# Fused attention blocks on one core: two slots instead of one between a pair's projection and its maxima

## The chip, the cores and the metric

The kernel runs on one core of a Trainium2 chip. The metric is device time in microseconds (us) of one execution. The engines carry these names in the profile: PE is TensorE (PEld its weight loads), DVE is VectorE, ACT is ScalarE, POOL is GpSimd, SP issues most DMAs.

## What is computed

The input `x` is 8 sequences of 256 rows by 160, the context 8 sequences of 512 rows by 96. A first block (an adapter with two attentions) is followed by a transformer block, cut here to what matters:

```
def cross_attention(x, ctx, wq, wk, wv, wo, bo):      # 20 heads of 64
    q, k, v = x @ wq, ctx @ wk, ctx @ wv              # split into heads
    attn = softmax(q @ k.T * 64 ** -0.5)
    return (attn @ v, heads joined) @ wo + bo

x = cross_attention(layer_norm(x), layer_norm(x), ...) + x    # "self": 256 keys
x = cross_attention(layer_norm(x), context, ...) + x          # "cross": 512 keys
x = geglu_ff(layer_norm(x)) + x
```

The weights of queries and keys are scaled so that the softmax needs its row maxima, and products are made of high and low parts to keep near float32 precision.

## The kernel before

`build` (L2271) runs stages one after the other: the adapter (two stages), `attention` for self (called at L2310), `attention` for cross (L2312), and `feed_forward`. The change touches only `attention` (L271) and the constant `TAIL` (L117).

`attention` treats the 8 batches in turn, and in each batch ten pairs of heads (`PAIRS`), one pair a slot. It is a software pipeline over slots. For pair `p` the steps are, each in its own slot: projection (`proj`, the queries, in self with the keys; `kproj`, the keys in cross, L753 to L770), maxima (`find_max`, L785 in cross and L790 in self: scores once, only to be reduced), `mt` (L850: the maxima transposed), `score` (L803 and L809: scores minus maxima, transposed, in high and low parts), and `weigh` (L829 to L831: probabilities times values in four groups, each one head and half of the rows). The line `MAX, MT, SCORE, WEIGH = 1, 2, 3, 4` (L284) says how many slots behind the projection each step comes. The slots of one batch run on into those of the next; `periods` (L98) writes out the kinds of batch: first, a hardware loop of six steady ones, two written out in each turn, last, and a tail of `TAIL` slots.

In self there are 256 keys and one round in a slot (`ROUNDS`, L281), in cross 512 keys and two. A round begins with `find_max` and `score` for their pairs; what follows is the list that `items` (L318) makes for a slot: (round, step). The extras that `extras` (L300) names are units of work that are not a pair's own: `ot` (L741, outputs of two pairs transposed), `out` (L750, L752: the output projection of half the rows), `v` (L735, a group of 512 or 256 value columns), `ctx` (L712, transposed context), `ln` (L718, transposed normalised rows of the next batch). `VALUES` (L296) places the `v` units. The first extra of a slot stands between weigh groups 0 and 1, the others between groups 2 and 3. In self both places are in the one round, in cross in the first and in the second.

The other engines walk the same lists in the same order:

- ACT (L559): exponentials (L567) of the scored round, then a copy of each unit's high part out of PSUM: `turned` (L557) for `mt`, `qk_h` (L552) for `proj` and `kproj`, `v_h` (L541), `attn_th` (L544), `ctx_h` (L537), and for `ln` the scaled rows (L521, L522).
- VectorE (L653): the reduction of the maxima (L664) first; in slot 4 the normalised rows `xn` of the next batch (`normalise`, L599 and L601, four pieces); then the low part of each unit: `qk_l` (L650), `v_l` (L629), `attn_tl` (L634), four operations for `ln` (L614 to L618), two additions for `out` (L641, L643); in slot 3 the statistics (L587 to L592); last the division of the weighed values by their sums (`recip` L680, `attn` L683).
- GpSimd (L483): in slot 4 the inverse root for the next batch (L473, L475) and the output bias (L488), then the low part of the probabilities (`probs_l`, L496), one operation a round.

What binds them are semaphores. `find_max` of a pair waits until VectorE has written its `qk_l` (`projected_by`, L349). The first weigh group waits for `probs_l` of its pair and for `attn` of the pair before, as they share a PSUM bank. The units `mt`, `proj`, `kproj` and all extras go through a ring of three shared PSUM banks (`Ring`, L40): a unit may start when the one three places before it has been read. `qk_h`, `qk_l` and `attn` keep four pairs (`KEPT`).

The order within a slot stands in this function:

```
if (s >= MT and cur) or (s < MT and kind != "first"):
    out.append((0, ("mt", s)))
if cur:
    out.append((0, ("proj", s)))
weigh = (s >= WEIGH and cur) or (s < WEIGH and kind != "first")
out += [(0, ("weigh", 0))] * weigh
out += [(0, key) for key in more[:1]]
out += [(0, ("weigh", 1))] * weigh
if cross and cur:
    out.append((last, ("kproj", s)))
```

Of the kernel before, what the change touches and what calls it, by code (L numbers as in the profile page):

```python
# [97 lines left out]
def periods(engine, slot):  # L98
# [11 lines left out]
    for s in range(PAIRS):  # L110
        slot("last", s, (NB - 1, 1), (NB - 2, 0), None)
    for s in range(TAIL):
        slot("tail", s, None, (NB - 1, 1), None)

TAIL = 7  # L117


def load_stacked(engine, out, w, semaphore):  # L120
# [150 lines left out]
def attention(nc, name, cross, x, ident, ctx_dram, weights, background):  # L271
# [9 lines left out]
    ROUNDS = KT // 2  # L281
    RB = ROUNDS * PAIRS

    MAX, MT, SCORE, WEIGH = 1, 2, 3, 4  # L284
    KEPT = 4

    def kept(parity, p):
# [12 lines left out]
    def extras(kind, s):  # L300

        out = []
        has_prev, has_nxt, has_cur = kind != "first", kind in ("first", "steady"), kind != "tail"
        if has_prev and s in (1, 2, 4):
            out.append(("ot", "prev", 2 + s // 2))
        if cross and has_nxt and s == 4:
            out.append(("ctx", "nxt", 0))
        if has_nxt and s == 4:
            out.append(("ln", "nxt", 0))
        if has_prev and s in (5, 6):  # L310
            out.append(("out", "prev", s - 5))
        if has_cur and s in (7, 9):
            out.append(("ot", "cur", s // 2 - 3))
        out += [("v", "nxt", v) for v in (VALUES[0].get(s, ()) if has_nxt else ())]
        out += [("v", "cur", v) for v in (VALUES[1].get(s, ()) if has_cur else ())]
        return out

    def items(kind, s):  # L318

        cur, more = kind != "tail", extras(kind, s)  # L320
        last = ROUNDS - 1
        out = []
        if (s >= MT and cur) or (s < MT and kind != "first"):
            out.append((0, ("mt", s)))
        if cur:
            out.append((0, ("proj", s)))
        weigh = (s >= WEIGH and cur) or (s < WEIGH and kind != "first")
        out += [(0, ("weigh", 0))] * weigh
        out += [(0, key) for key in more[:1]]
        out += [(0, ("weigh", 1))] * weigh  # L330
        if cross and cur:
            out.append((last, ("kproj", s)))
        out += [(last, ("weigh", 2))] * weigh
        out += [(last, key) for key in more[1:]]
        out += [(last, ("weigh", 3))] * weigh
        return out

    def all_keys(kind):
        if kind == "tail":
            return [key for s in range(TAIL) for _, key in items(kind, s) if key[0] != "weigh"]  # L340
        pre = []
        if kind == "first":
            pre = [("ctx", "pre", 0)] * cross + [("ln", "pre", 0)] + [("v", "pre", v) for v in range(AHEAD)]
        return pre + [key for s in range(PAIRS) for _, key in items(kind, s) if key[0] != "weigh"]
# [18 lines left out]
    with stack:  # L363
# [153 lines left out]
        def _(act):  # L517
# [41 lines left out]
            def slot(kind, s, cur, prev, nxt):  # L559
                period = cur[0] if cur is not None else NB  # L560
                for r in range(ROUNDS):
                    if (work := before(s, SCORE, cur, prev)) is not None:
                        (b, _), p = work
                        n = p * ROUNDS + r
                        act.wait_ge(scored, b * RB + n + 1)
                        after(act, pv_done, b * PAIRS + p - 1)
                        nc.scalar.activation(probs[:, n % PR, :, :].rearrange("p j k -> p (j k)"), score_bank[:, :], ACT.Exp,  # L567
                                             scale=SCALE).then_inc(exped, 1)
                    for at, key in items(kind, s):
                        if at != r or key[0] == "weigh":  # L570
                            continue
                        if key[0] == "mt":
                            turn_shift(kind, period, key, before(s, MT, cur, prev))
                        elif key[0] in ("proj", "kproj"):
                            projected(kind, s, cur, key)
                        else:
                            extra(kind, period, key, {"cur": cur, "prev": prev, "nxt": nxt}[key[1]])
# [1693 lines left out]
def build(nc, columns, shapes, a, out):  # L2271
# [5 lines left out]
    with stack:  # L2277
        x = stack.enter_context(nc.sbuf_tensor("x_rows", [P, NT, HID], F32))
        ident = stack.enter_context(nc.sbuf_tensor("ident", [P, P], F32))
        with ExitStack() as self_stack:  # L2280
            self_weights = SelfWeights(nc, self_stack, {w.rstrip("1"): l1[w] for w in ("g1", "be1", "wq1", "wk1", "wv1", "wo1", "bo1")})
            with ExitStack() as adapter_stack:
# [25 lines left out]
                adapter(nc, x, const, context, raw, branch)  # L2308
            cross_weights = CrossWeights(nc, stack, {w.rstrip("2"): l1[w] for w in ("g2", "be2", "wq2", "wk2", "wv2", "bo2")})
            attention(nc, "self", False, x, ident, context, self_weights, cross_weights)  # L2310
        late = LateRaw(nc, stack, {"wo": l1["wo2"], "w1": l1["w_ff1"]})
        attention(nc, "cross", True, x, ident, context, cross_weights, late)  # L2312
        feed_forward(nc, x, ident, l1["g3"], l1["be3"], l1["b_ff1"], l1["b_ff2"], l1["w_ff2"], late, out)

# [14 lines left out]
```

## Time and profile before

| | us |
|---|---|
| median of 3 runs | 1677.85 (1672.35 to 1679.42) |
| the profiled execution, its own time | 1676.27 |
| its span | 1674.5 |
| mean granted clock of TensorE, share of full | 0.939 |
| busy: PE, PEld | 1465.7 (88%), 1236.4 (74%) |
| busy: DVE, ACT, POOL | 1101.1 (66%), 747.4 (45%), 734.6 (44%) |

The self-attention lies between about 436 and 884 us of the span, the cross-attention between 884 and 1563, the feed-forward behind it. The time of an execution is 1.8 us more than the span of its profile.

How to read the rows: a timeline row is start, duration, engine, line, operation, what is written from what, the shape and the count of instructions merged, and in brackets how long the engine had been idle and whom it waited for. A wait row names the waiting engine and line, the releaser, the total, the number of times and the longest. A window row gives the busy us of each engine with its number of instructions, then the granted clock. A matmul's duration is longer than the distance to the next one, since they are pipelined; distances are taken from start to start.

### The profile page before, as it was taken

Reading aid. Unit: us, or ns where it says so; the run is one execution under the profiler, and the core shown is the slowest. Engines: PE = TensorE matmul, PEld = TensorE weight load, DVE = VectorE, ACT = ScalarE, POOL = GpSimd, SP = SyncE. Lnnn points to the kernel's source line nnn. Section 1 sums busy time; section 2 is a strip of 40 time slices with the busy share of each in tenths; the row PEclk is TensorE's granted clock in tenths of the full one; section 3 lists DMA queues with packets and bytes.
Section 4 is the critical chain, followed back from the end, with each engine's and each line's share of the span. In section 5 each row is a group of like instructions: output and inputs, shape, how many; then the busy total and the mean of one; then the engine's idle time right before and its main releaser. Section 6 shows DMA issues by size and latency. Waiting matters only on the chain. (4 is left out here: it accounts for less than half of the span.)

```text
span 1674.5 us, 42467 instructions
## 1 busy us (share of the span) xinstructions
PE 1465.7 (88%) x16742; PEld 1236.4 (74%) x16742; DVE 1101.1 (66%) x2091; ACT 747.4 (45%) x1365; POOL 734.6 (44%) x576
## 2 busy tenths in 40 slices
PE   4786899999589999899986999999998999998487
PEld 3564777777478888788875788878887888887477
DVE  3773677776467766767646776766685767665376
ACT  0442344444244544445532554545454545554243
POOL 1341355556444443434432554544454545445154
PEclk9865899999799999999997999999999999999699
DMA  3110000000200000000001000000000000000000
GB/s 94 48 37 12 9 7 10 5 1 2 57 1 2 2 2 2 2 2 2 2 2 34 7 2 7 6 3 3 7 24 18 2 2 2 2 2 2 12 13 20
DMA packets 23427, 19.51 MB, mean 12 GB/s; under 512 B 12962, under 2 KB 21638, under 8 KB 23238
## 3 DMA queue, kind: packets, MB, share of 16 engines
q1 hardware_dynamic: 23238, 16.83, 3.8%
q8 instruction: 139, 2.28, 0.5%
q14 instruction: 50, 0.41, 0.1%
HBM read 15.51 MB, written 1.31 MB: 10 GB/s over the span
## 5 line engine op out<-in xcount | busy, mean ns | idle before, releaser
L496 POOL TENSOR_TENSOR cross_probs_l<-cross_probs 128x1024 f16<-128x1024 f32 x160 | 303.3, 1896 | 337.2 <-ACT cross_probs L567 337.2
L567 ACT ACTIVATE cross_probs<-cross_score 128x1024 f32<-128x1024 f32 x160 | 164.0, 1025 | 278.3 <-PE cross_score L809 278.3
L496 POOL TENSOR_TENSOR self_probs_l<-self_probs 128x1024 f16<-128x1024 f32 x80 | 151.6, 1895 | 242.1 <-ACT self_probs L567 242.0
L664 DVE TENSOR_REDUCE cross_maxima<-cross_max 128x2 f32<-128x1024 f32 x160 | 195.0, 1219 | 10.1 <-PE cross_max L785 7.9
L1982 POOL TENSOR_TENSOR ad_probs_l<-ad_probs 128x512 f16<-128x512 f32 (+1 forms) x128 | 133.7, 1045 | 124.1 <-ACT ad_probs L2028 123.8
L650 DVE TENSOR_TENSOR cross_qk_l<-cross_shared,cross_qk_h 128x256 fp32r<-128x256 f32 (+1 forms) x160 | 89.0, 556 | 122.4 <-ACT cross_qk_h L552 122.3
L829 PE MATMUL cross_pv<-cross_v_h,cross_probs 128*128 128x65 bf16 x1280 | 149.8, 197 | 7.6 <-DVE cross_attn L683 4.3
L829 PEld LDWEIGHTS cross_pv<-cross_v_h,cross_probs 128*128 128x128 bf16 x1280 | 116.9, 98 | 46.7 <-issue 37.9
L830 PE MATMUL cross_pv<-cross_v_l,cross_probs 128*128 128x64 f16 x1280 | 147.3, 194 | 0.0
L831 PE MATMUL cross_pv<-cross_v_h,cross_probs_l 128*128 128x65 bf16 x1280 | 146.6, 194 | 0.0
L567 ACT ACTIVATE self_probs<-self_score 128x1024 f32<-128x1024 f32 x80 | 82.3, 1029 | 141.9 <-PE self_score L809 141.9
L830 PEld LDWEIGHTS cross_pv<-cross_v_l,cross_probs 128*128 128x128 bf16 x1280 | 120.0, 99 | 0.5
L2028 ACT ACTIVATE ad_probs<-ad_score 128x512 f32<-128x512 f32 (+1 forms) x128 | 76.5, 598 | 97.8 <-PE ad_score L2219 97.8
L831 PEld LDWEIGHTS cross_pv<-cross_v_h,cross_probs_l 128*128 128x128 f16 x1280 | 119.9, 99 | 0.0
L785 PE MATMUL cross_max<-cross_qk_h 64*128 64x512 f32 x320 | 80.6, 500 | 31.9 <-DVE cross_qk_l L650 25.8
L650 DVE TENSOR_TENSOR self_qk_l<-self_shared,self_qk_h 128x512 fp32r<-128x512 f32 x80 | 55.2, 690 | 71.0 <-ACT self_qk_h L552 71.0
L664 DVE TENSOR_REDUCE self_maxima<-self_max 128x4 f32<-128x1024 f32 x80 | 97.3, 1217 | 3.7 <-PE self_max L790 3.5
L809 PE MATMUL cross_score<-cross_qk_h 64*128 64x256 f32 x640 | 92.1, 281 | 0.0
L809 PE MATMUL cross_score<-cross_qk_l,cross_qk_h 64*128 64x256 f32 x640 | 92.1, 281 | 0.0
L809 PE MATMUL cross_score<-cross_qk_h,cross_qk_l 64*128 64x256 f32 x640 | 91.8, 279 | 0.0
L2103 DVE TENSOR_REDUCE ad_maxima<-ad_max 128x1 f32<-128x508 f32 x128 | 84.2, 681 | 3.6 <-PE ad_max L2205 1.9
L829 PE MATMUL self_pv<-self_v_h,self_probs 128*128 128x65 bf16 x640 | 78.9, 197 | 6.9 <-DVE self_attn L683 6.7
(441 smaller groups left out, 5042.6 us busy)
## 6 DMA issues: line engine op xcount, KB each, us to landing
ad_ctx_rows<-in_ctx SPq DMA_DIRECT2D x8, 192.0 KB, 2.6
cross_ctx_rows<-in_ctx SPq DMA_DIRECT2D x8, 192.0 KB, 2.6
x_rows<-in_x SPq DMA_DIRECT2D x1, 1280.0 KB, 6.3
sw_raw<-in_L_xattn_wq SPq DMA_DIRECT2D x2, 640.0 KB, 6.0
sw_raw<-in_L_xattn_wk SPq DMA_DIRECT2D x2, 640.0 KB, 3.7
sw_raw<-in_L_xattn_wv SPq DMA_DIRECT2D x2, 640.0 KB, 3.6
cw_raw<-in_L_xattn_wq SPq DMA_DIRECT2D x2, 640.0 KB, 4.6
lr_raw<-in_L_xattn_w_ff SPq DMA_DIRECT2D x2, 640.0 KB
```

The lines of the kernel that those rows point to most:

```text
L496: nc.gpsimd.tensor_tensor(probs_l[:, n % PR, :, :].rearrange("p j k -> p (j k)"), whole, whole.bitcast(BF16)[:, 1::2], ALU.subtract).then_ ...
L567: nc.scalar.activation(probs[:, n % PR, :, :].rearrange("p j k -> p (j k)"), score_bank[:, :], ACT.Exp, scale=SCALE).then_inc(exped, 1)
L650: nc.vector.tensor_tensor(qk_l[:, kept(parity, s), at:at + width], shared[ring.bank(kind, key)][:, 0:width], qk_h[:, kept(parity, s), at:a ...
L664: nc.vector.reduce_max(out, scores, AX.X).then_inc(max_read, 1)
L785: mm = nc.tensor.matmul(max_bank[:, j * 512:(j + 1) * 512], qk_h[half, at, r * P:(r + 1) * P], qk_h[half, at, SEQ:SEQ + KD], start=True, s ...
L809: mm = nc.tensor.matmul(score_bank[:, j * 512 + c * SEQ:j * 512 + (c + 1) * SEQ], ks[half, at, keys], qs[half, at, 0:SEQ], start=False, st ...
L829: nc.tensor.matmul(pv_bank[:, at:at + DV], hi, v_h[parity][:, c, head, :], start=c == 0, stop=False)
L830: nc.tensor.matmul(pv_bank[:, at:at + DH], hi, v_l[parity][:, c, head, :], start=False, stop=False)
L831: mm = nc.tensor.matmul(pv_bank[:, at:at + DV], lo, v_h[parity][:, c, head, :], start=False, stop=last)
L1982: nc.gpsimd.tensor_tensor(probs_l[rows, n % PR, :], whole, whole.bitcast(BF16)[:, 1::2], ALU.subtract).then_inc(probs_split, 1)
L2028: nc.scalar.activation(probs[rows, n % PR, :], score_bank[n % 2][rows, :], ACT.Exp, scale=SCALE).then_inc(exped, 1)
L2103: nc.vector.reduce_max(maxima[:, v % 2, step % 2, at:at + 1], max_bank[n % 2][:, 0:KEYS], AX.X).then_inc(max_read, 1)
```

## The change

The distances become 2, 3, 4 and 5, so that every step behind the projection comes a slot later, and the tail has eight slots. The extras `ot` and `out` move to the slots in which their pairs are now ready; `ctx`, `ln` and the `v` units keep their slots. In `items` the projection `proj` moves from the place behind `mt` to the one ahead of weigh group 2, in cross into the second round, ahead of `kproj`. The whole diff:

```diff
--- before.py
+++ after.py
@@ -114,7 +114,7 @@
 
 
 
-TAIL = 7
+TAIL = 8
 
 
 def load_stacked(engine, out, w, semaphore):
@@ -281,7 +281,7 @@
     ROUNDS = KT // 2
     RB = ROUNDS * PAIRS
 
-    MAX, MT, SCORE, WEIGH = 1, 2, 3, 4
+    MAX, MT, SCORE, WEIGH = 2, 3, 4, 5
     KEPT = 4
 
     def kept(parity, p):
@@ -301,16 +301,16 @@
 
         out = []
         has_prev, has_nxt, has_cur = kind != "first", kind in ("first", "steady"), kind != "tail"
-        if has_prev and s in (1, 2, 4):
-            out.append(("ot", "prev", 2 + s // 2))
+        if has_prev and s in (2, 3, 5):
+            out.append(("ot", "prev", (s + 3) // 2))
         if cross and has_nxt and s == 4:
             out.append(("ctx", "nxt", 0))
         if has_nxt and s == 4:
             out.append(("ln", "nxt", 0))
-        if has_prev and s in (5, 6):
-            out.append(("out", "prev", s - 5))
-        if has_cur and s in (7, 9):
-            out.append(("ot", "cur", s // 2 - 3))
+        if has_prev and s in (6, 7):
+            out.append(("out", "prev", s - 6))
+        if has_cur and s in (8, 9):
+            out.append(("ot", "cur", s - 8))
         out += [("v", "nxt", v) for v in (VALUES[0].get(s, ()) if has_nxt else ())]
         out += [("v", "cur", v) for v in (VALUES[1].get(s, ()) if has_cur else ())]
         return out
@@ -322,14 +322,14 @@
         out = []
         if (s >= MT and cur) or (s < MT and kind != "first"):
             out.append((0, ("mt", s)))
-        if cur:
-            out.append((0, ("proj", s)))
         weigh = (s >= WEIGH and cur) or (s < WEIGH and kind != "first")
         out += [(0, ("weigh", 0))] * weigh
         out += [(0, key) for key in more[:1]]
         out += [(0, ("weigh", 1))] * weigh
-        if cross and cur:
-            out.append((last, ("kproj", s)))
+        if cur:
+            out.append((last, ("proj", s)))
+            if cross:
+                out.append((last, ("kproj", s)))
         out += [(last, ("weigh", 2))] * weigh
         out += [(last, key) for key in more[1:]]
         out += [(last, ("weigh", 3))] * weigh
```

In slot 4 of a steady batch the lists of steps behind maxima and scores become, in self: before `mt, proj, weigh 0, ot 4, weigh 1, weigh 2, ln, weigh 3`, after `mt, weigh 0, ln, weigh 1, proj, weigh 2, weigh 3`; in cross: before `mt, proj, weigh 0, ot 4, weigh 1 | kproj, weigh 2, ctx, ln, weigh 3`, after `mt, weigh 0, ctx, weigh 1 | proj, kproj, weigh 2, ln, weigh 3`, where | divides the rounds.

## Rows read from the trace of the kernel before

**Rows 1.** busy us (count) of each engine in one self batch, then granted clock
```profile
core 0: us, PE busy (x) PEld busy (x) DVE busy (x) ACT busy (x) POOL busy (x), PEclk, DMA share, GB/s
541.09:592.66 51.57, 47.99 (x610) 43.24 (x610) 36.52 (x69) 25.80 (x43) 20.70 (x14) 1.00 0.01 2
```

**Rows 2.** who waited for whom: us in total, times, longest; whole run
```profile
PE cross_max L785 <- DVE cross_qk_l L650: 25.8, 38, 1.8
...
PE self_shared L718 <- DVE self_xn L601: 18.7, 8, 5.2
...
PE self_max L790 <- DVE self_qk_l L650: 15.2, 30, 1.4
...
PE self_pv L829 <- DVE self_attn L683: 6.7, 8, 1.5
```

**Rows 3.** timeline of TensorE, self-attention, slots 3 to 5 of one batch; columns named
```profile
start us, us, engine line op out<-in xcount [idle before <-releaser]
...
566.61 0.28 PE L757 MATMUL self_shared<-self_ln_h,sw_wk_s 128*128 128x256 f32 x1
...
568.37 0.51 PE L790 MATMUL self_max<-self_qk_h 64*128 64x256 f32 x4 [0.73 <-DVE self_qk_l L650]
...
569.94 0.37 PE L757 MATMUL self_shared<-self_ln_h,sw_wq_h 128*128 128x256 f32 x1
...
573.58 0.65 PE L718 MATMUL self_shared<-ident,self_xn 128*128 128x128 f32 x4 [1.44 <-DVE self_xn L601]
...
577.89 0.19 PE L829 MATMUL self_pv<-self_v_h,self_probs 128*128 128x65 bf16 x1 [0.81 <-DVE self_attn L683]
```

**Rows 4.** timeline of VectorE, the same slots
```profile
567.54 0.69 DVE L650 TENSOR_TENSOR self_qk_l<-self_shared,self_qk_h 128x512 fp32r<-128x512 f32 x1 [0.97 <-ACT self_qk_h L552]
...
569.15 0.42 DVE L683 TENSOR_TENSOR self_attn<-self_pv,self_recip 128x256 f32<-128x256 f32 x1
...
570.96 1.98 DVE L601 TENSOR_SCALAR self_xn<-x_rows,self_mean_var,self_rstd 128x128 f32 x1
...
577.32 0.42 DVE L683 TENSOR_TENSOR self_attn<-self_pv,self_recip 128x256 f32<-128x256 f32 x1
```

**Rows 5.** timeline of TensorE, first tail slot of the self-attention
```profile
861.26 0.50 PE L790 MATMUL self_max<-self_qk_h 64*128 64x256 f32 x4 [0.18 <-DVE self_qk_l L650]
...
862.91 0.19 PE L829 MATMUL self_pv<-self_v_h,self_probs 128*128 128x65 bf16 x1
```

**Rows 6.** timeline of both engines, self slot after one that ends in a V group
```profile
550.98 0.50 PE L790 MATMUL self_max<-self_qk_h 64*128 64x256 f32 x4
...
551.51 0.69 DVE L629 TENSOR_TENSOR self_v_l<-self_shared,self_v_h 128x512 f16<-128x512 f32 x1 [0.68 <-ACT self_v_h L541]
...
552.32 0.42 DVE L683 TENSOR_TENSOR self_attn<-self_pv,self_recip 128x256 f32<-128x256 f32 x1
```

**Rows 7.** timeline of both engines, the same place in the cross-attention
```profile
1312.85 0.50 PE L785 MATMUL cross_max<-cross_qk_h 64*128 64x512 f32 x2
...
1313.98 0.42 DVE L683 TENSOR_TENSOR cross_attn<-cross_pv,cross_recip 128x256 f32<-128x256 f32 x1
```

**Rows 8.** timeline of GpSimd, slot 4 of rows 3
```profile
570.96 1.89 POOL L496 TENSOR_TENSOR self_probs_l<-self_probs 128x1024 f16<-128x1024 f32 x1
```

**Rows 9.** timeline of both engines, cross-attention, slots 4 and 5
```profile
1078.04 0.50 PE L785 MATMUL cross_max<-cross_qk_h 64*128 64x512 f32 x2 [0.30 <-DVE cross_qk_l L650]
...
1079.15 0.42 DVE L683 TENSOR_TENSOR cross_attn<-cross_pv,cross_recip 128x256 f32<-128x256 f32 x1
...
1083.65 0.67 DVE L634 TENSOR_TENSOR cross_attn_tl<-cross_shared,cross_attn_th 128x512 fp32r<-128x512 f32 x1
...
1086.18 0.49 PE L785 MATMUL cross_max<-cross_qk_h 64*128 64x512 f32 x2 [0.75 <-DVE cross_qk_l L650]
...
1088.56 0.42 DVE L683 TENSOR_TENSOR cross_attn<-cross_pv,cross_recip 128x256 f32<-128x256 f32 x1
...
1089.13 0.19 PE L829 MATMUL cross_pv<-cross_v_h,cross_probs 128*128 128x65 bf16 x1 [0.63 <-DVE cross_attn L683]
```

**Rows 10.** windows as in rows 1: a pause of TensorE and what follows it
```profile
602.50:605.10 2.60, 0.15 (x5) 0.03 (x1) 1.20 (x3) 0.58 (x1) 0.00 (x0) 0.99 0.00 0
605.10:608.50 3.40, 3.33 (x23) 3.02 (x23) 1.23 (x1) 0.71 (x1) 0.00 (x0) 0.51 0.02 5
```

## The prediction

> **What bounds the kernel now.** I read the page's busy shares first, then the table of windows, the waits, and the timelines of single slots. In one batch of the self-attention TensorE is busy 47.99 of 51.57 us at full clock, VectorE 36.5, GpSimd 20.7 [rows 1]; the batches in the middle of a stage repeat each other to a few hundredths, so one slot read closely stands for its sisters. TensorE sets the time, but only where it does not wait, and its waits have three names [rows 2]. For the maxima of a pair it waits for VectorE's low parts (`qk_l`, L650) of the projection issued one slot earlier: 15.2 us in 30 waits in self, 25.8 us in 38 in cross. For the transposes of the next batch's normalised rows (`ln` unit, L718) it waits for VectorE's L601: 18.7 us, 8 times. For the first weigh group it waits for VectorE's `attn` of the pair before: 6.7 us, 8 times in self.
>
> Slot 4 of a self batch shows all three [rows 3]: maxima at 568.37 after 0.73 us idle, the `ln` transposes at 573.58 after 1.44, the next slot's first weigh at 577.89 after 0.81. VectorE is the releaser each time [rows 4]: `qk_l` ends at 568.23, `attn` at 569.57, the second `xn` piece takes from 570.96 to 572.94, `attn` of slot 4 ends at 577.74. So VectorE's order inside slots 3 to 5 is a chain as tight as TensorE's.
>
> **What the change removes.** With two slots between projection and maxima, `qk_l` is ready a whole slot ahead. The two rows together are 41.0 us. Start to start a wait costs a little more: after the last projection matmul at 566.61, the 24 weigh matmuls (0.03 us each) and two hand-overs of 0.12 would put the maxima at 567.56, so 0.81 is lost where the row says 0.73. Scaled so, the gain is **46 us** (bounds 41 and 48); about 9 of it lies in the two stage starts.
>
> **What it adds: the weigh group comes sooner.** TensorE's matmuls are the same in number, but the order in a slot changes from mt, proj, weigh to mt, weigh, proj. Today the projection (about 1.0 us in self: eight matmuls from 569.94 to the weigh) covers VectorE's `attn` of the slot before. Now nothing does. The tail of self already has the new order: maxima at 861.26, first weigh at 862.91, 1.65 us later [rows 5]; with a projection next it starts 1.57 us after the maxima (568.37 to 569.94). When can `attn` be ready? Where a 512-wide V group is last in a slot, slot start 550.98, `v_l` from 551.51, `attn` ends at 552.74: 1.76 us, and 0.15 more to the weigh (577.74 to 577.89), so 1.91 against 1.57: **0.34** lost in two slots of a self batch. Where the projection is last, its last matmul starts 1.62 us before `qk_l` ends (566.61, 568.23), `attn` ends 0.54 after the DVE operation ahead of it (552.20 to 552.74 [rows 6]), plus 0.15: 2.31 after that matmul; TensorE needs 0.12 + 0.36 + 0.09 + 1.57 = 2.14 from it, so **0.17** in some four slots. With 0.13 and 0.08 for the two others outside slots 3 to 5, a self batch pays 1.6 us: 6 x 1.6 and 2.9 for the first and last batch are **12.5 us**. Below nothing is excluded, since no matmul goes; the upper end is 20 if every slot paid 0.3. In cross the V-last case is milder: slot start 1312.85, `attn` ends at 1314.40, 1.55 + 0.15 against 1.56: 0.14 in four slots [rows 7]; the key projection is followed by twice the weigh work and waits for nothing; the five other slots pay the changed hand-over of 0.09. That is 1.0 us a batch, **8 us** in all (0 to 12).
>
> **The `ln` unit is moved, though the diff doesn't name it.** `ot` unit 4 goes from slot 4 to slot 5. In self `ln` was the second extra of slot 4, after weigh 2; now it is the first and goes right behind weigh 0, before the projection. VectorE's chain to `xn` does not get shorter: `qk_l` of slot 3, statistics, GpSimd's root, reduce, four normalising pieces, one of them held for 1.98 us beside GpSimd's `probs_l`, which starts at the same 570.96 [rows 4, 8]. Count from E, the end of slot 3's projection (566.89): `attn` ends at E+2.68, `ln` can start at E+6.69. After the change slot 4 starts at E+0.29, its first weigh is due at E+1.86 and comes at E+2.83 (0.97 lost), and `ln` is due at E+3.01 and comes at E+6.69: 3.68 lost where 1.61 is now. Behind it stand weigh 1, the projection, weigh 2 and 3 and all of slot 5. On VectorE `ln` now stands before the projection's low part: from `ln` to the end of `attn` it is 4.16 now (573.58 to 577.74) and 4.76 with 0.6 of `qk_l` between, so slot 5's weigh comes at E+11.6 against a due time of E+10.33: 1.27 lost, 0.97 now. Together 0.97 + 2.07 + 0.30 = 3.34 us a batch, six steady batches, and 0.5 in the first: **20.5 us** (bounds 10, should only the `ln` wait grow and by what the moved `ot` and projection took, 0.55 + 1.0; and 25).
>
> In cross `ctx` takes the first place and `ln` stays behind weigh 2, where `xn` is long ready, so that wait doesn't come. But the q projection's low part moves into the second round, VectorE's chain in slot 4 loses only `ot` (0.6), and TensorE arrives earlier. `attn` of slot 3 ends at 1079.57, the weigh may start at 1079.72; the slot would start 0.38 before 1078.04, the weigh is due at 1079.22: 0.5. `attn` of slot 4 would end at 1088.38 instead of 1088.98, the weigh comes at 1088.53; TensorE, 0.8 us of wait and `ot`'s 0.44 shorter, is due some 1.9 earlier. 0.5 + 1.9 against what stands now before 1089.13 (0.63 in the row, 0.8 start to start) is +1.6 a batch, **10.5 us** over six and the first [rows 9] (5 to 13).
>
> **Queues passed.** ACT copies in the new order and has no late item; the shared banks are claimed three units back, and every such bank was emptied before `attn`, which is waited for anyhow: nothing. No DMA moves. The tail grows by one slot in each attention, its matmuls taken from the slot before; the bubbles of one thin slot, 1 us each (0.3 to 1.7, by the waits of the present tails): **2 us**.
>
> **The clock.** After TensorE's pause of 2.6 us (602.50 to 605.10) its granted clock is 0.51 for the next 3.4 us, which is the 1.2 GHz level [rows 10]. The new pause at `ln` is 0.97 and 3.68 us with one weigh group of 0.18 between. At half clock 3.4 us lose 1.7 us, most of it inside the 1.27 that slot 5 waits anyway: 0.5 a batch, **3 us** (0 to 16). The Trainium skill, page TensorE: Matmul & The Clock Gate, section Why this matters for your kernels, says that idle gaps between bursts put the clock back to its low level; by that rule each of these pauses would be followed by slow matmuls, which is the rival below.
>
> **Sum.** -46 + 12.5 + 8 + 20.5 + 10.5 + 2 + 3 = +10.5 on the profiled execution's 1676.27. The gains in the stage starts are the least certain and I put them 2 higher, since two slots without maxima also ease VectorE: 1684.8. The median shown is 1.6 above the profiled execution, so 1685 to 1686; I take **1685**. About 0.5% (8 us) is what a measurement of this kernel can tell from no change.
>
> **Rivals.**
> *Slower, by the clock.* Place: the `ln` unit in slot 4 of each self batch. If the pause there pulls the clock down and slot 5 runs at the low level too, past its slack of 1.27, each of six batches pays some 2 us more: 1685 + 12 = 1697. For it speaks that a shorter pause does it now [rows 10]; against it that the present pauses at `ln` don't, and that much of the slow time is covered. It decides if the pause reaches about 2.6 us. Chance 0.24.
> *Faster, by a missed collision.* The long `xn` piece and `probs_l` both start at 570.96 [rows 4, 8]. If after the change VectorE's piece starts first, it takes a third of a us instead of 1.98, and both chains of slot 4 shorten by 1.65 in 12 batches: 1685 - 20 = 1665. Against it: both engines are released by the same statistics, so their distance stays. The Trainium skill, page SBUF — State Buffer, section Who interferes with whom, says that whichever engine starts first holds the shared ports for its whole instruction and the other blocks; by that rule this near tie could fall either way. Chance 0.15.
> *The whole gain.* VectorE keeps up everywhere and only 46 - 8 us remain: 1638. Rows 4 and 9 speak against it. Chance 0.04.
> *The forecast*, 1677 to 1693, has 0.57: its bounds are the terms' ends taken half-way.
>
> **Numbers.** Of the forecast's 0.57 some 0.34 lies within 0.5% and 0.23 above; the clock's 0.24 is slower; of the collision's 0.15, 0.11 is faster and 0.04 same; the whole gain is faster. That is 0.15 faster, 0.38 same, 0.47 slower. The range 1668 to 1700 holds the forecast and the clock's rival and leaves out the whole gain and about half of the collision's.
>
> **What would show it.** The maxima's waits for `qk_l` go to nearly nothing. L718's wait in self rises from 18.7 to about 35 us, the weigh's wait for `attn` from 6.7 to over 20 in self, and by 15 or more in cross. A self batch takes about 54.9 us instead of 51.57, a cross batch half a us to one more. I am wrong if L718 waits no longer than now, if self batches get shorter, or if the clock column drops in every batch.

## The result and the profile after

The kernel after takes 1681.76 us (median of 20 runs, 1676.31 to 1688.69) where the one before, run beside it, takes 1674.55 (20 runs, 1666.05 to 1681.0): a ratio of 1.0043, with a 95% interval of 1.0029 to 1.0057. That is slower by 0.43%, inside the 0.5% that the prediction called no change. The profiled execution took 1677.53 us, its span 1675.7, against 1676.27 and 1674.5: it is one of the quick ones of the kernel after, so the two profiles lie 1.3 us apart where the medians lie 7.2 apart. From its page, the busy times and the granted clock:

```profile
PE 1487.7 (89%) x16742; PEld 1247.4 (74%) x16742; DVE 1097.7 (66%) x2091; ACT 747.5 (45%) x1365; POOL 733.9 (44%) x576
...
PEclk9995899999799999999997899999999999999799
```

Nearly equal totals hide two stages that moved against each other. A stage is read here from its first `ln` transposes (self) or the end of self (cross) to its last output addition (L643); a batch is the distance from the `ln` unit (L718) of one batch to that of the next, taken within one turn of the hardware loop.

| us | before | after | difference |
|---|---|---|---|
| self stage | 444.7 | 460.0 | +15.3 |
| one self batch | 51.7 | 55.5 | +3.8 |
| cross stage | 682.9 | 668.1 | -14.8 |
| one cross batch | 79.9 | 78.9 | -1.0 |

The rest of the profile, adapter and feed-forward, differs by 0.8 us. A stage total is that of one execution and carries a few us of chance (the same self took 464.5 in e1 below, the same cross 672.3 in e2); a batch inside a turn of the loop repeats to 0.2 us in these two kernels, and one that crosses a turn is 2 to 6 us longer. Where in a stage the difference arises, from the starts of the `ln` units:

| us, after minus before | start | steady batches | end |
|---|---|---|---|
| self (start: to the second `ln`; end: from the last) | -7.0 | +17.4 | +4.9 |
| cross (start: to the third `ln`; end: from the last) | -9.9 | -2.7 | -2.2 |

So two thirds of what cross gains lies in its first batches and not in the steady ones: there eight waits for `qk_l`, 6.5 us, are gone, and one wait of a V unit for `v_l` fell from 5.0 to 1.5. In self the start gains 7.0, with four waits for `qk_l`, 4.3 us in all, shrunk to one of 0.5. The batches as windows (columns as in [rows 1]), first of the kernel before:

```profile
629.21:680.92 51.71, 48.11 (x608) 43.27 (x609) 36.51 (x69) 25.81 (x43) 20.70 (x13) 1.00 0.01 2
1170.11:1250.02 79.91, 76.72 (x997) 65.00 (x995) 56.44 (x96) 41.18 (x70) 39.62 (x24) 1.00 0.02 4
```

and of the kernel after:

```profile
629.85:685.32 55.47, 51.12 (x608) 45.12 (x609) 36.66 (x68) 25.22 (x43) 20.63 (x13) 0.96 0.01 1
1175.47:1254.42 78.95, 76.68 (x1000) 64.68 (x996) 56.41 (x96) 41.67 (x71) 39.58 (x24) 1.00 0.03 6
```

The work is the same (matmul counts agree to a few records). In self TensorE's busy time grew by 3.0 at a clock of 0.96; in cross it did not grow and the idle time shrank from 3.2 to 2.3. The waits of the kernel after, to be held against [rows 2]:

```profile
PE self_shared L718 <- DVE self_xn L601: 29.7, 8, 4.9
PEld self_shared L718 <- issue: 21.3, 6, 3.6
PEld self_pv L829 <- issue: 18.5, 58, 0.9
...
PE cross_pv L829 <- issue: 8.9, 6, 1.5
...
PE self_pv L829 <- DVE self_attn L683: 6.1, 8, 1.5
```

Both `qk_l` rows of [rows 2], 41.0 us, are gone. The wait for `xn` rose from 18.7 to 29.7. The weigh's wait for `attn` did not rise by name in self; the weight loads' "issue" did, from 13.5 in 34 waits to 18.5 in 58, and in cross there are six pauses of 1.5 that bear no name. That is how this page shows a wait whose releaser it can't tie to the instruction: the timeline has to say whose it is. TensorE in slots 4 and 5 of a self batch, then VectorE and GpSimd in the same slots, as in [rows 3, 4, 8]:

```profile
566.32 0.50 PE L790 MATMUL self_max<-self_qk_h 64*128 64x256 f32 x4
...
568.84 0.19 PE L829 MATMUL self_pv<-self_v_h,self_probs 128*128 128x65 bf16 x1 [0.71 <-DVE self_attn L683]
...
572.62 1.11 PE L718 MATMUL self_shared<-ident,self_xn 128*128 128x128 f32 x4 [3.44 <-DVE self_xn L601]
...
577.95 0.19 PE L829 MATMUL self_pv<-self_v_h,self_probs 128*128 128x65 bf16 x1
```

```profile
570.05 1.93 DVE L601 TENSOR_SCALAR self_xn<-x_rows,self_mean_var,self_rstd 128x128 f32 x1
...
577.42 0.42 DVE L683 TENSOR_TENSOR self_attn<-self_pv,self_recip 128x256 f32<-128x256 f32 x1
```

```profile
570.00 1.89 POOL L496 TENSOR_TENSOR self_probs_l<-self_probs 128x1024 f16<-128x1024 f32 x1
```

The weigh waits 0.71, the `ln` transposes wait 3.44, and the first weigh of slot 5 waits for nothing that is marked: TensorE itself comes late, since the four transposes took 1.11 us where they take 0.65 in [rows 3]. The windows around them (columns as before) show the pause and the clock:

```profile
568.30:572.70 4.40, 0.42 (x7) 0.33 (x8) 4.19 (x6) 0.80 (x2) 3.52 (x4) 0.94 0.00 0
572.70:576.10 3.40, 3.40 (x30) 3.28 (x30) 1.23 (x3) 1.26 (x3) 0.00 (x0) 0.58 0.00 0
576.10:578.50 2.40, 2.40 (x34) 1.98 (x31) 2.32 (x6) 1.22 (x2) 0.00 (x0) 1.00 0.01 3
```

A granted clock near 0.5 is the 1.2 GHz level; before the fall TensorE had paused 3.44 us. In cross, the same places as [rows 9]:

```profile
1085.70 0.19 PE L829 MATMUL cross_pv<-cross_v_h,cross_probs 128*128 128x65 bf16 x1 [0.68 <-DVE cross_attn L683]
...
1094.45 0.19 PE L829 MATMUL cross_pv<-cross_v_h,cross_probs 128*128 128x65 bf16 x1 [1.49 <-issue]
```

Elsewhere in a cross batch the first weigh group starts 1.64 to 1.73 us behind the slot's first maxima, so it loses at most 0.09 us.

### The profile page after: what moved, and what is told of

The parts are those of the page before. It is cut to its first block and busy times, and to the rows that moved or that the text cites. A ratio compares the mean times of both kernels' runs of the same rounds, so it can differ in the third digit from the quotient of the medians.

```text
span 1675.7 us, 42451 instructions
## 1 busy us (share of the span) xinstructions
PE 1487.7 (89%) x16742; PEld 1247.4 (74%) x16742; DVE 1097.7 (66%) x2091; ACT 747.5 (45%) x1365; POOL 733.9 (44%) x576
## 5 line engine op out<-in xcount | busy, mean ns | idle before, releaser
L829 PE MATMUL self_pv<-self_v_h,self_probs 128*128 128x65 bf16 x640 | 87.2, 198 | 7.3 <-DVE self_attn L683 6.1
```

Of the source, the lines that this page charges most:

```text
L829: nc.tensor.matmul(pv_bank[:, at:at + DV], hi, v_h[parity][:, c, head, :], start=c == 0, stop=False)
```

## The experiments

Ratios are to the kernel before, run on the same chip. "Self" and "cross" are the stages and batches as defined above.

| run | median | ratio [95%] | self, batch | cross, batch |
|---|---|---|---|---|
| e1 change in self only | 1692.18 | 1.0098 [1.0071, 1.0125] | 464.5, 55.5 | 685.7, 79.9 |
| e2 change in cross only | 1662.53 | 0.9922 [0.9895, 0.9948] | 443.6, 51.7 | 672.3, 79.0 |
| e3 self's `ln` back | 1671.66 | 0.9987 [0.9966, 1.0008] | 453.7, 54.4 | 669.2, 78.9 |
| e4 self's projection back | 1656.25 | 0.9882 [0.9857, 0.9907] | 443.3, 52.2 | 669.8, 79.0 |
| e5 e4, statistics earlier | 1659.95, one run | none | 435.1, 50.4 | 675.8, 79.0 |
| e6 e5, normalising first | 1639.32 | 0.9784 [0.9763, 0.9806] | 412.3, 47.9 | 671.8, 79.6 |
| e7 before, with e6's moves | 1664.38 | 0.9921 [0.9898, 0.9943] | 431.5, 50.0 | 686.4, 80.0 |
| e8 after, with e6's moves | 1664.31 | 0.9922 [0.9900, 0.9943] | 440.7, 52.1 | 676.4, 79.5 |
| e9 e6's moves in self only | 1633.91 | 0.9763 [0.9736, 0.9789] | 413.9, 47.9 | 671.4, 78.9 |
| e10 both projections back | 1696.48 | 1.0146 [1.0115, 1.0177] | 440.0, 52.2 | 710.3, 83.3 |
| e11 e6, `ln` ahead of `ctx` | 1633.81 | 0.9765 [0.9736, 0.9795] | 415.2, 47.9 | 671.7, 78.3 |
| e12 e9, q behind `mt`, 5 kept | 1627.72 | 0.9720 [0.9696, 0.9743] | 415.4, 47.9 | 664.4, 78.3 |

A cross stage differs between profiles by a few us with an equal batch (668.1 to 675.8 at 78.9 to 79.0), by pauses at the turns of the hardware loop and at its first batch. So a claim about cross rests on the batch, and its total only where the difference is larger.

**e1 and e2, the two halves alone.** The distances, extras, tail and order follow a switch:

```diff
-    MAX, MT, SCORE, WEIGH = 2, 3, 4, 5
+    FAR = not cross          # e2: FAR = cross
+    TAIL = 8 if FAR else 7
+    MAX, MT, SCORE, WEIGH = (2, 3, 4, 5) if FAR else (1, 2, 3, 4)
```

> The change made in the self-attention alone, the cross-attention as before. Stage lengths in the two traces: self 444.7 us before and 460.0 after, cross 682.9 and 668.1. My theory (two separate effects that cancel): self stays at 460 (459 to 461), cross at 683, the whole some 15 us over the kernel before, ratio about 1.009. Rival (the stages share a cause, such as code placement or the clock): self comes out well under 460 or cross moves by more than 3 us though nothing in it is edited.

> The change made in the cross-attention alone, the self-attention as before. My theory: self 445 us, cross 668 us (667 to 670), the whole some 15 us under the kernel before (about 1660, ratio 0.991). Rival: the gain in cross is an effect of what self left behind, and cross stays over 675.

Self alone is slower by 1.0%, cross alone faster by 0.8%: the whole change is the sum of two clear effects of opposite sign (the product of the ratios is 1.0020, which the intervals do not part from 1.0043). The batches are those of the kernel after whatever the other attention does, 55.5 and 79.0. The stage totals missed the ranges expected: self 464.5 where 459 to 461 was, cross 672.3 where 667 to 670 was, and in e1 the unedited cross came out 2.8 longer. So such a total is not to be read closer than 5 us.

**e3, the moved `ln` unit.** Only self's `ln` goes back behind weigh 2:

```diff
+        if more and more[0][0] == "ln":
+            more = [None] + more
-        out += [(0, key) for key in more[:1]]
+        out += [(0, key) for key in more[:1] if key]
```

> The changed kernel with the ln unit of self put back behind weigh 2, where it stood before. My theory: the normalised rows come when VectorE's chain has them, so TensorE's total wait in slots 4 and 5 is set by that chain; what is won is the 0.6 us of the projection's low part that stood between ln and attn, and some 0.4 us of half-clock matmuls: 1.0 us in each of six steady batches, a batch 54.5 instead of 55.5, self 454 (452 to 456). Rival (the position of ln costs the whole 2.1 us of longer wait): 3 us a batch, self 442. Second rival (the clock's drops are the loss, 17 us more at half clock in self): they vanish and self falls by 8 or 9.

The pause before `ln` fell from 3.44 to 2.06 us and the batch by 1.1. So the place of `ln` alone is worth some 6 us of the stage; the rest of self's loss is elsewhere. The clock still fell after some of these pauses, though not after all. Windows behind the `ln` of two batches, each after a pause of 2.06 to 2.08 us:

```profile
678.10:681.50 3.40, 3.40 (x30) 3.02 (x30) 2.06 (x5) 1.19 (x3) 0.00 (x0) 0.63 0.00 0
734.38:737.80 3.42, 2.58 (x30) 2.10 (x30) 2.09 (x5) 2.18 (x4) 0.06 (x1) 1.00 0.00 0
```

The fall cost this kernel nothing: its batches inside a turn take 54.45 and 54.33 us with a fall (`ln` at 511.05 and 623.77) and 54.44 without (at 734.38). In the last, the first weigh of slot 5 waits 1.69 us for `attn`; where the clock fell it waits 0.29 to 0.46, since TensorE comes to it later.

**e4, the order of projection and weigh in self.** Self's `proj` returns to the place behind `mt`, the distances stay:

```diff
+        if cur and not cross:
+            out.append((0, ("proj", s)))
...
         if cur:
-            out.append((last, ("proj", s)))
+            if cross:
+                out.append((last, ("proj", s)))
             if cross:
                 out.append((last, ("kproj", s)))
```

> The changed kernel with self's projection put back behind mt, ahead of the weigh groups; cross as changed. It covers attn again and puts 1.0 us of matmuls ahead of ln. My theory: the small waits of the weigh groups (0.14 to 0.27 us in seven slots) go, 1.4 us in each of eight batches, and the ln wait falls by 1.0 to 1.4 us in six: self 460 to about 441 (438 to 446), a steady batch 52.7. Rival (the small waits were bought from elsewhere, since the maxima or the banks then wait instead): self stays over 452.

One batch:

```profile
619.07:671.31 52.24, 49.03 (x609) 44.64 (x609) 36.58 (x69) 25.70 (x43) 20.63 (x13) 0.96 0.01 2
```

3.3 us a batch come back, 17 in the stage (441 was expected, 443.3 came). The late projection is the dearest part of the change in self. The small losses ahead of weigh 0 are gone in the slots outside 3 to 5; the `ln` pause is still 3.2 us and the clock still falls behind it.

**e5 and e6, VectorE's chain to `xn`.** e5 adds to e4 the statistics in slot 2 and the inverse root in slot 3, e6 also moves the four normalising pieces ahead of slot 4's reduction of the maxima, both in both attentions:

```diff
-                if s == 4 and nxt is not None:
+                if s == 3 and nxt is not None:
                     inverse_root(nxt[0])
...
-                if s == 3 and nxt is not None:
+                if s == 2 and nxt is not None:
                     statistics(nxt[0])
...
                 for r in range(ROUNDS):
+                    if s == 4 and r == 0 and nxt is not None:      # e6
+                        normalise(nxt[0])
                     if (work := before(s, MAX, cur, prev)) is not None:
...
-                    if s == 4 and r == 0 and nxt is not None:      # e6
-                        normalise(nxt[0])
```

> The kernel of e4_proj_first with VectorE's statistics moved from slot 3 to slot 2 and GpSimd's inverse root from slot 4 to slot 3; the four normalising pieces stay behind the reduction of slot 4. My theory (what holds the rows back is the piece that stands still beside GpSimd's probs_l, not the statistics): VectorE reaches the pieces earlier, but probs_l starts about 2.5 us into the slot and runs 1.9, so one piece of about 1.9 us stays and the ln wait of 3.1 us falls by 0.3 only (0 to 0.8): self 441 (437 to 443). Rival (the length of the chain counts): the wait falls by the 1.7 us that the chain is shorter, self 431.

> As e5_pf_early, with the four normalising pieces also put ahead of the reduction of slot 4, where GpSimd is not yet at probs_l. My theory: no long piece is left in self, the ln wait of 3.1 us goes to under 0.5, and in cross VectorE's chain in slot 4 is short enough that the 1.65 us wait of slot 5's weigh goes: self 425 (422 to 430), cross 656 (652 to 661), the whole about 1625. Rival (VectorE's order merely passes the wait on to the reduction, attn or the maxima): self stays over 435.

e5 gained 1.8 a batch, more than the theory and less than the rival: one piece still took 1.92 us beside `probs_l`. Here a fall of the clock does cost: the batches inside a turn take 51.40 us with one (`ln` at 513.57) and 50.41 and 50.42 without (at 620.57 and 726.38), and slots 3 to 5 take 16.6 to 16.7 in three batches with a fall (`ln` at 513.57, 564.97 and 670.98) and 15.74 in the two without. The first weigh of slot 5 waits only 0.4 us without a fall, so little of the slow stretch is covered. In e6 all pieces are short. Its VectorE and GpSimd:

```profile
557.21 0.34 DVE L602 TENSOR_SCALAR self_xn<-x_rows,self_mean_var,self_rstd 128x128 f32 x1
557.46 0.34 DVE L604 TENSOR_SCALAR self_xn<-x_rows,self_mean_var,self_rstd 128x128 f32 x1
557.72 0.34 DVE L602 TENSOR_SCALAR self_xn<-x_rows,self_mean_var,self_rstd 128x128 f32 x1
557.97 0.34 DVE L604 TENSOR_SCALAR self_xn<-x_rows,self_mean_var,self_rstd 128x128 f32 x1
```

```profile
556.44 0.87 POOL L491 TENSOR_TENSOR x_rows<-x_rows,sw_bo_row 128x320 f32 x1
558.46 1.89 POOL L499 TENSOR_TENSOR self_probs_l<-self_probs 128x1024 f16<-128x1024 f32 x1 [1.15 <-ACT self_probs L570]
```

But for 0.1 us the pieces fall between two operations of GpSimd's, and they end 0.15 us before `probs_l` starts. The Trainium skill, page SBUF — State Buffer, section Who interferes with whom, has VectorE and GpSimd share a port pair that the first to start holds; the 1.93 against 0.34 us of the same piece, with and without `probs_l` beside it, agree. Self's batch, 47.9, has 0.4 us of idle time left:

```profile
608.76:656.65 47.89, 47.49 (x614) 43.21 (x611) 34.76 (x69) 25.68 (x44) 20.66 (x14) 1.00 0.01 2
```

That is far better than the 425 us expected (412.3). In cross the expectation (656) was wrong: the batch got 0.6 longer. The pieces now delay the reduction that the second round's maxima wait for: that wait of TensorE's rose from 2.9 us in the kernel after to 8.0.

**e7 and e8, the same moves without e4's order.** They separate the moves from the change: e7 makes them in the kernel before, e8 in the kernel after.

> The kernel before (one slot between projection and maxima) with the same move of statistics, inverse root and normalising pieces as e6_pf_norm. My theory: the ln wait (1.61 us a batch) and most of the attn wait of slot 5 (0.97) go, the waits for qk_l stay: self 432 (430 to 436), cross 672 (668 to 676). Rival (with the chain out of the way one slot of distance is as good as two): self and cross come within 3 us of e6_pf_norm.

> The changed kernel, with nothing put back but the same move of statistics, inverse root and normalising pieces. It says how much of the changed kernel's loss hung on VectorE's chain to the rows. My theory: of 5.9 us of waits in self's slots 4 and 5 some 2.6 are left, 3.3 less in six batches, self 460 to 440 (436 to 445); in cross 2.5 us a batch less, 668 to 654 (650 to 660); the drops of the granted clock at ln vanish. Rival (the small waits of the weigh groups and the clock's drops carry the loss): self stays over 450.

Self came as expected in both (431.5 for 432, 440.7 for 440). Cross missed in both: 686.4 where 672 was expected and 676.4 where 654 was, and neither batch became shorter. In e8 the `ln` pause is 0.67 us and the clock stays at 1.00 in the six batches behind it. Compared at like clocks, e8 (52.1) and e6 (47.9) price the late projection in self at 4.2 a batch; at the old distances self's best is 50.0 (e7), at the new ones with the old order 47.9. So the two slots between projection and maxima are worth 2.1 a batch in self once nothing else stands in VectorE's way. The order that the change brings along takes twice that back. (e4 gave 3.3 for the same order, with VectorE's chain to `xn` still long; that the chain took the difference is argued, not shown.)

**e9, the moves in self only.** The conditions of e6 with `cross` excepted.

> The kernel after with self's projection behind `mt` again and, in self alone, the early statistics and inverse root and the normalising pieces ahead of the reduction; cross is the change's, untouched. My theory: the two attentions are independent, so self is that of e6 (412 us, batch 47.9) and cross that of the kernel after (668, batch 78.9, 0.5 a batch less than in e6 and e8, where the moved pieces delay cross's own chain). 1639 minus about 3: near 1635, ratio to before 0.976. Rival: cross's half a us in e6 and e8 was chance of the runs; then the time is e6's, 1639 or more.

It came at 1633.91, expected near 1635. The batch of cross is 78.9 again, so the 0.6 of e6 was of the moves; the whole differs from e6 by 0.2%, within the intervals.

**e10, both projections back.** Cross's q projection too stands behind `mt`.

```diff
+        if cur:
+            out.append((0, ("proj", s)))
...
         if cur:
-            out.append((last, ("proj", s)))
             if cross:
                 out.append((last, ("kproj", s)))
```

> The kernel after with the projection behind `mt` again in both attentions; against e4 only cross's q projection goes back into the first round. It prices the later projection in cross. By my prediction's terms (8 us for weigh groups that come sooner, and the part of the 10.5 in slots 4 and 5 that comes from the q projection's low part in the second round) cross should fall from 669 to 655 to 662, the whole to 1643 to 1650. Rival, by the gaps read in the trace after, where cross's weigh groups outside slots 4 and 5 wait for nothing: no more than the share of slots 4 and 5, 0.3 to 0.9 a batch, so cross 663 to 668 and the whole 1650 to 1656.

Both theories fell: cross took 710.3, forty more than e4. Its waits name why:

```profile
DVE cross_qk_l L651 <- ACT cross_qk_h L553: 229.0, 72, 7.4
ACT cross_qk_h L553 <- PE cross_score L810: 207.8, 76, 4.4
...
PE cross_max L786 <- DVE cross_maxima L665: 41.7, 45, 1.3
```

and its ScalarE, then its VectorE, in one slot:

```profile
1025.88 0.37 ACT L558 CAST cross_turned<-cross_shared 128x256 fp32r<-128x256 f32 x1
1028.31 0.37 ACT L553 CAST cross_qk_h<-cross_shared 128x256 fp32r<-128x256 f32 x1 [2.07 <-PE cross_score L810]
```

```profile
1028.72 0.42 DVE L651 TENSOR_TENSOR cross_qk_l<-cross_shared,cross_qk_h 128x256 fp32r<-128x256 f32 x1 [2.25 <-ACT cross_qk_h L553]
...
1029.81 1.22 DVE L665 TENSOR_REDUCE cross_maxima<-cross_max 128x2 f32<-128x1024 f32 x1
```

`qk_h` keeps four pairs (`KEPT`), and ACT may overwrite pair p - 4 only when both rounds of its scores are done (L550). With `SCORE` at 4 these scores are in the same slot, the last of them in the second round. A projection in the first round must stand still for them on ACT, and VectorE's second reduction stands behind its low part. So in cross the move of the projection into the second half is not a choice of balance: with four pairs kept the longer distance needs it.

**e11, `ln` ahead of `ctx` in cross.**

```diff
-        if cross and has_nxt and s == 4:
-            out.append(("ctx", "nxt", 0))
         if has_nxt and s == 4:
             out.append(("ln", "nxt", 0))
+        if cross and has_nxt and s == 4:
+            out.append(("ctx", "nxt", 0))
```

> e6 with `ln` ahead of `ctx` in slot 4 of cross, so that VectorE's four operations for `ln` stand in the first round and only one operation for `ctx` stands ahead of `attn`. My theory: the 1.6 us that the first weigh group of slot 5 waits in cross is the four operations of `ln` (1.7 us) that stand between the key projection's low part and `attn`; with 1 us less there the wait falls to about 0.6 and cross by 6 to 8 us, from 671.8 to about 665. Rival: the wait comes from VectorE's whole amount of work in slots 4 and 5 (maxima 2.4, projection 1.1, ln 1.7, ctx 0.7, attn 0.6); then it moves elsewhere in the slot (the second maxima) and cross stays at 672.

The batch fell from 79.6 to 78.3, the upper end of the 1.0 to 1.3 that the expected 6 to 8 us need, so the place is right: VectorE's four operations for `ln` ahead of `attn`. The stage did not fall in this profile (671.7): the stretch behind the last `ln` is 4.8 us longer than in e6, and no run here tells why. The whole is 0.2% below e6, within the intervals. The stage total stays undecided.

**e12, five pairs of queries kept.** e9 with cross's q projection behind `mt`, and

```diff
+            q_h = sb("q_h", [P, 5, SEQ], F32R)
+            q_l = sb("q_l", [P, 5, SEQ], F32R)
...
-                after(act, scored, b * RB + (s - KEPT + 1) * ROUNDS)
+                after(act, scored, b * RB + (s - (5 if cross and key[0] == "proj" else KEPT) + 1) * ROUNDS)
...
-        attn_tl = sb("attn_tl", [P, NCH, SEQ], F32R)
+        attn_tl = sb("attn_tl", [P, NCH - cross, SEQ], F32R)
```

> e9 with cross's q projection back behind `mt`, as in e10, but with five pairs of queries kept in place of four (the keys stay at four). The fourth pair from the end of the low parts of the output projection is given up for the room in SBUF: in cross the low parts of pairs 8 and 9 are written over those of pairs 7 and 8, so that part of the result is left out; no instruction is left out. My theory: e10's 40 us came from ACT, which may copy the queries of pair p only when pair p - 4 is scored, and with three slots between them that score is in the second round of the same slot; ACT waited 207.8 us in 76 waits, and VectorE's second reduction stood behind it. With five kept the wait goes and cross falls from e10's 710 (batch 83.3) to that of the change or below: by my prediction's terms for cross (weigh groups 1.0 a batch, and 0.9 of slots 4 and 5 for the low part in the second round) a batch of 77.0 to 78.0, cross 657 to 664, the whole about 1622 to 1628. Rival one, from the gaps in the trace of the kernel after: only slots 4 and 5 gain, up to 0.8 a batch, cross 665 to 669, whole 1628 to 1633. Rival two: the kept pairs are not the cause, and cross stays near 700.

One cross batch of e10, then of e12:

```profile
1168.24:1251.57 83.33, 77.30 (x995) 65.15 (x995) 54.51 (x96) 39.91 (x71) 39.59 (x23) 1.00 0.02 4
```

```profile
1125.16:1203.50 78.34, 76.67 (x995) 64.87 (x995) 56.33 (x96) 41.36 (x71) 39.62 (x24) 1.00 0.02 6
```

5.0 a batch come back and ACT's wait for scores is gone: the kept pairs were the cause of e10. Against the order of the change (78.9) the batch gains 0.6, by the first of the two rivals that the expectation names, not the 0.9 to 1.9 of my terms: from maxima to maxima slot 4 is 0.33 longer and slot 5 0.80 shorter than in e9, and none of the eight others differs by more than 0.05. So the late projection costs cross little but what it does to slots 4 and 5. The totals don't decide this: stage and whole (664.4 and 1627.72) lie between the theory's ranges and the rival's. This kernel, 1627.72 us or 2.8% below the one before, gives up part of the result; the best with the whole result are e9 and e11, at 0.976.

## Why the prediction was right, and where it was not

The time, 1681.76 against 1685, came out, and with it the forecast's place within 0.5% of the kernel before; but the chances that stood beside it gave 0.47 to slower than that and 0.38 to the same. The mechanisms are those forecast, with one term of the wrong size and one reason that failed. That the medians differ by 7.2, where the forecast's difference was 7, is in part luck, as the sum below shows. Point by point:

- **The waits for `qk_l`** went as forecast. What they were worth is seen in cross, where little else changed: -2.83 start to start in a steady batch (0.37, 0.80 and twice 0.83).
- **The `ln` unit of self** was right in kind and size. 0.97 was forecast ahead of the first weigh of slot 4 and 3.68 ahead of `ln`. Counted as the forecast counts, from 1.57 behind the maxima (566.32 to 568.84) and from 0.18 behind the weigh (568.84 to 572.62), they are 0.95 and 3.60. Only the statement for the page was off: the wait rose to 29.7, not "about 35", and the step's own 2.07 in six batches on 18.7 gives 31.
- **The weigh term of self**, 1.6 a batch, holds. From maxima to maxima the seven slots outside 3 to 5 are longer in e8 than in e6 by 0.37, 0.18, 0.14, 0.20, 0.37, 0.24 and 0.24: 1.7 (the forecast's own terms count eight such slots). Slots 3 to 5 add 0.8, 1.0 and 0.6. But it does not stand under `attn` in the waits (forecast over 20, 6.1 came); it is "issue" and busy time. In cross the row was to grow by 15 or more: by name it is 4.1 where it was 4.3, and the six pauses without a name add 8.9.
- **The clock**: "I am wrong if the clock column drops in every batch". It did, in all six steady batches, as the rival had it. The rule of the Trainium skill that stood beside it (TensorE: Matmul & The Clock Gate, Why this matters for your kernels) speaks of long idle gaps alone, which the prediction left out. The falls behind 3.44 us here and 3.20 in e4, six of six each, agree with it; those behind 2.06 to 2.08 us in e3 and 2.35 in e5, four of six each, are behind shorter gaps than it names, and there the measurement decides. Yet the rival's price, 12 us, did not come. The slow stretch of 3.4 us lies where slot 5 would have waited for `attn` anyhow: with the first weigh at 577.95 and `attn` done at 577.84 the expected wait of 1.27 is gone. By the forecast's count from the same maxima this weigh was due at 577.63, so it comes 0.3 late: the drop took the place of a wait, and the forecast's small term held while its reason (that most batches keep their clock) failed. No run changes the clock alone, but e3 and e5 have batches with and without a fall, and they agree: where slot 5's first weigh has 1.69 us to wait a fall costs nothing (e3), where it has 0.4 a fall costs 0.8 to 1.0 (e5). In the kernel after the clock fell in all six batches, so for it this is argued. What a fall can have cost there is the 0.46 us by which the four transposes took longer, 1.11 for 0.65, as VectorE's way to `attn` leads over them.
- **The weigh term of cross**, 8 us, is the mis-sized term. Outside slots 4 and 5 the first weigh group loses 0.09 at most. The prediction took 0.14 in four slots and 0.09 for the hand-over in five others, 1.0 a batch; e12 prices the whole order of cross at 0.6 a batch, slots 4 and 5 included.
- **Slots 4 and 5 of cross**: forecast +1.6, measured 0.85, 0.18 and 1.65 in place of 0.81, which is +1.9. With -2.83 that is -0.9 a batch, and -1.0 is measured. The text, though, said that a cross batch takes "half a us to one more": its own terms, 1.0 + 1.6 and the -2.83, give -0.2. That sentence was not worked out from the sum.
- **The sum.** By the profiled stages self lost 15.3 and cross gained 14.8, where the terms make cross gain 8 to 10 (26 to 29 us of `qk_l` less 8 and 10.5) and self lose about 20 (12.5, 20.5, 3 and a tail, less 17 of `qk_l`). In these two profiles both were off by some 5 in the same direction, so the total, forecast at +8.5 on the profile, came at +1.3. In e1 and e2 the same attentions come out at +19.8 and -10.6, about as forecast, and the medians differ by +7.2: a good part of the 5 is the chance of one execution, and how near the time came is partly luck.
- **The stage starts**, put at about 9 and then 2 more, brought more: 7.0 in self and 9.9 in cross (6.9 in e1, 6.2 in e2), 13 to 17 in all. The wait of a V unit for `v_l` at the start of cross, 5.0 before and 1.5 after, stands in no term. Against this, the end of self grew by 4.9, and how that divides into the weigh term, slots 4 and 5 and the longer tail no run here shows.
- **The missed collision** did not happen: the second piece took 1.93 us and starts 0.05 after `probs_l`. Its price was right, and e6 shows that the way to it is to move the pieces, not to hope for the order of a near tie.
- Not seen at all: that `KEPT` ties the place of the projection to the distance (e10). It cost the prediction nothing, since the change keeps to it; "ACT has no late item" was true only for that reason.

## What to carry to other kernels

Moving a step later in a software pipeline buys slack at one wait and takes cover from others: list what the moved instructions used to hide (here `attn` and the chain to `xn`), and price each. When a pipeline gets longer, check every buffer that keeps a fixed number of items; a step that was free may now wait for one in its own slot. And a whole that hardly moves may be two halves that cancel: run each alone before judging the idea. Here one half was worth 0.8%; the other was worth 1% once its order was restored and VectorE's chain shortened (self 413.9 in e9 against 431.5 in e7, which has the same moves at the old distances).

## What was unexpected of the hardware

The clock's fall is not decided by the length of the pause alone. Idle time of TensorE before `ln` in the self batches behind the first, and in how many of six the clock fell to 1.2 GHz within 2 us of their end:

| kernel | pause, us | clock fell |
|---|---|---|
| before | 1.42 to 1.44 | 0 of 6 |
| e8 | 0.67 | 0 of 6 |
| e3 | 2.06 to 2.08 | 4 of 6 |
| e5 | 2.34 to 2.35 | 4 of 6 |
| e4 | 3.20 to 3.21 | 6 of 6 |
| after | 3.43 to 3.44 | 6 of 6 |

Two batches of e5, behind pauses of 2.35 us each, in the windows' columns:

```profile
564.97:568.40 3.43, 3.43 (x34) 3.17 (x36) 1.65 (x4) 1.02 (x2) 0.00 (x0) 0.53 0.01 2
620.57:624.00 3.43, 3.43 (x48) 3.18 (x49) 2.10 (x5) 1.83 (x3) 0.00 (x0) 1.00 0.00 0
```

In the same 3.43 us TensorE did 34 matmuls at the low level and 48 at the high one. The batches run the same instructions, so what differs is the moment; what sets it no run here shows. What a fall costs depends on what waits behind it: by the batches of e3 and e5 compared above, nothing in the one and 0.8 to 1.0 us in the other.
